# A four-block vision kernel on one core: normalisations of three chunks merged, another order in the third pass, and three products by high and low parts

## What is computed

```python
xn = layernorm(x, ln1_w, ln1_b)
xs = jnp.roll(xn, shift=(-SHIFT, -SHIFT), axis=(1, 2))      # SHIFT = 3
xw = xs.reshape(B, H // WS, WS, W // WS, WS, C)             # windows of WS x WS = 7 x 7 = 49 tokens
xw = xw.transpose(0, 1, 3, 2, 4, 5).reshape(-1, N, C)
qkv = xw @ qkv_w + qkv_b
qkv = qkv.reshape(-1, N, 3, NH, hd).transpose(2, 0, 3, 1, 4)   # 6 heads of 16
q, k, v = (qkv[0], qkv[1], qkv[2])
attn = jax.nn.softmax(jnp.einsum('bhqd,bhkd->bhqk', q, k) * scale, axis=-1)
o = jnp.einsum('bhqk,bhkd->bhqd', attn, v)
o = o.transpose(0, 2, 1, 3).reshape(-1, N, C)
o = o @ proj_w + proj_b
...
x = shortcut + o
h = layernorm(x, ln2_w, ln2_b)
h = jax.nn.gelu(h @ mlp_w1 + mlp_b1, approximate=False)     # 96 -> 384 -> 96
x = x + (h @ mlp_w2 + mlp_b2)
```

## Time and profile before

| | us |
|---|---|
| median of 3 runs | 12922.99 |
| lowest, highest | 12919.95, 12924.1 |
| the profiled execution: its own time | 12924.79 |
| the profiled execution: span of the trace | 12922.7 |
| its mean granted PE clock | 0.985 of full |

### The profile page before, as it was taken

One profiled execution on the slowest core, in us unless ns is written; L12 is line 12 of the kernel. 1 busy time (PEld: TensorE's weight loads), 2 busy tenths in 40 slices (PEclk: granted clock), 3 DMA queues, 4 the chain that ended last, 5 costly groups with the idle time before them and its releaser, 6 DMA issues. The chain is left out here.

```text
span 12922.7 us, 343424 instructions
## 1 busy us (share of the span) xinstructions
PE 11843.0 (92%) x135956; PEld 7144.1 (55%) x135956; DVE 7256.5 (56%) x12102; ACT 8898.6 (69%) x15550; POOL 308.8 (2%) x772
## 2 busy tenths in 40 slices
PE   6999998999999999999888888888899999999999
PEld 3444443555555555556755555555566666666665
DVE  4444444666666666663455555655555555555555
ACT  4555554888888888884355555555677777777777
POOL 0000000000000000000000000000000000000000
PEclk9999998999999999999999999999899999999999
DMA  1111111222222222225522222222000000000000
...
DMA packets 1103863, 593.29 MB, mean 46 GB/s; under 512 B 864651, under 2 KB 1076566, under 8 KB 1099704
## 3 DMA queue, kind: packets, MB, share of 16 engines
...
...
## 5 line engine op out<-in xcount | busy, mean ns | idle before, releaser
L964 PE MATMUL banks<-L_VB,L_PT 113*49 113x34 f32 x36864 | 1086.4, 214 | 294.5 <-ACT L_PT L1117 294.5
L964 PEld LDWEIGHTS banks<-L_VB,L_PT 113*49 113x49 f32 x36864 | 1007.1, 126 | 618.1 <-issue 618.1
L913 PEld LDWEIGHTS banks<-L_ident,L_PR 113*113 113x113 f32 x9216 | 1116.8, 179 | 340.9 <-issue 246.9
L913 PE MATMUL banks<-L_ident,L_PR 113*113 113x113 f32 x9216 | 1280.0, 270 | 3.2 <-ACT L_PR L1133 2.6
L985 PE MATMUL banks<-L_XN,L_W 97*128 97x392 f32 x3072 | 1243.5, 514 | 3.2 <-ACT L_Y L1164 1.5
L908 PE MATMUL banks<-L_SQ,L_J 96*96 96x392 f32 x2560 | 1095.6, 509 | 142.6 <-ACT L_SQ L1106 142.6
L1117 ACT COPY L_PT<-banks 113x452 f32<-113x452 f32 x1792 | 947.2, 529 | 375.4 <-PE banks L913 369.0
L378 PE MATMUL banks<-scan_XS,scan_W1T 97*96 (+1 forms) x2688 | 1112.4, 552 | 0.0
L1133 ACT ACTIVATE L_PR<-L_SX 113x588 f32<-113x588 f32 x1536 | 1088.6, 709 | 16.4 <-DVE L_SX L1260 10.7
L1057 PE MATMUL banks<-L_Hd,L_W 128*97 128x392 f32 x3072 | 1099.1, 493 | 0.0
L1111 ACT ACTIVATE L_LV<-banks,L_eps 96x392 f32<-96x392 f32 x1280 | 747.1, 584 | 430.5 <-PE banks L908 430.5
...
## 6 DMA issues: line engine op xcount, KB each, us to landing
...
after_L<-L_X SPq DMA_DIRECT2D x512, 147.0 KB
...
L_norm_by_phase<-L_XP SPq DMA_DIRECT2D x512, 84.0 KB, 2.2
...
L_norm<-L_XA SPq DMA_DIRECT2D x256, 147.0 KB, 2.0
...
L_XR<-L_norm SPq DMA_DIRECT2D x256, 147.0 KB, 2.2
```

What stands on the lines that cost most here:

```text
L913: mm = pe.transpose(bank(TURN[a])[0:SPAN, (k % 4) * SPAN:(k % 4 + 1) * SPAN], PR[:, st.v if lag else st.u, 2 * k:2 * k + 2, :].rearrange(" ...
L964: mm = pe.matmul(bank(HEADS_BANK)[p0:p0 + TOK, col:col + VW], PT[:, st.v, q // 2 * G + g, p0:p0 + TOK], VB[:, st.v, q, g, :], start=True, ...
```

## The change

1. The normalisations of a step are merged. `variances` multiplies the squares of chunk t+1 (X), t-2 (X1) and, in L1, t-3 (X2) by a 96 x 32 `J`, in pieces of 98 columns, and leaves each mean on 32 rows of its own of one bank; ACT takes one Ln and one Exp of all of them (`rstd`); `spread` multiplies each group of 32 rows by `PICK` (one row of ones) and puts it on 96 rows of three banks; DVE multiplies from there (`normalised`). XN is thus made one step ahead.
2. The squares go from ACT to POOL (`square_rows`, and SQ2 and SQ3 in `step`), and so does XA. POOL runs now in L3 too.
3. Keys, queries and the first MLP layer are computed by parts: x and the weights are each split into a high part, rounded to the format float32r, and the rest; three float32r matmuls (high x high, high x low, low x high) add up in the bank. The weights are split once (`split_weights`), the activations by POOL: a cast and a subtraction each for XN and XN2. The convolution pass had such matmuls already.
4. The order of the steps of L1 and L3 is another one: heads come ahead of the hidden blocks, keys and queries at the step's start, values behind `spread`.
5. In L2 DVE adds both halves of the bias first, and the second subtraction comes behind the sums; on PE the second and third `turn` stand together ahead of the values, the turned heads no longer wait for the queries' copy and come ahead of the convolution's product, and the scores wait for `biased1` in place of `centred1`; ACT copies both PT groups ahead of the values.

```diff
+def split_weights(nc, name, parts):
+            @block.vector
+            def _(dve):
+                for whole, high, low in parts:
+                    dve.tensor_copy(high.bitcast(F32R), whole).then_inc(rounded, 1)
+                dve.wait_ge(rounded, len(parts))
+                for whole, high, low in parts:
+                    dve.tensor_tensor(low.bitcast(F32R), whole, high, ALU.subtract)
...
-                def variance(sq, k, ready):
-                    pe.matmul(bank(k)[0:C, 0:CH], J[:], sq, start=True, stop=True).then_inc(s[ready], 1)
+                def norms(st):
+                    nx = st.ahead()
+                    return ([(0, SQ[:, nx.u])] if nx.f else []) + ([(1, SQ2[:, st.u])] if st.m else []) + ([(2, SQ3[:, st.v])] if st.n and kind == "L1" else [])
+                def variances(st):
+                    if st.ahead().f:
+                        st.ahead().wait("sq", 0)
+                    if st.m:
+                        st.wait("sq2", 2)
+                    if st.n and kind == "L1":
+                        st.wait("sq3", 3)
+                    if st.k:
+                        st.wait("centred1", 1)
+                    for k in range(PAIRS):
+                        cols = slice(2 * TOK * k, 2 * TOK * (k + 1))
+                        for g, sq in norms(st):
+                            mm = pe.matmul(bank(VAR_BANK)[NORM_ROWS * g:NORM_ROWS * (g + 1), cols], J[:], sq[:, cols], start=True, stop=True)
+                    mm.then_inc(s["variances"], 1)
+                def spread(st):
+                    st.wait("rstd", -1)
+                    for k in range(PAIRS):
+                        cols = slice(2 * TOK * k, 2 * TOK * (k + 1))
+                        for g, _ in norms(st):
+                            rows = slice(NORM_ROWS * g, NORM_ROWS * (g + 1))
+                            mm = pe.matmul(bank(NORM_BANK[g])[0:C, cols], PICK[rows], RS[rows, st.u, cols], start=True, stop=True)
+                    mm.then_inc(s["spread"], 1)
...
+                def by_parts(out, wh, wl, xh, xl):
+                    for n, (wt, xt) in enumerate(((wh, xh), (wh, xl), (wl, xh))):
+                        mm = pe.matmul(out, wt.bitcast(F32R), xt.bitcast(F32R), start=(n == 0), stop=(n == 2))
+                    return mm
...
+                    out = bank(K_BANK)[0:C, 0:CH]
                     if mlp:
-                        st.wait("centred1", 1)
-                    pe.matmul(bank(K_BANK)[0:C, 0:CH], Wk[0:C + 1, :], XN[:, st.u], start=True, stop=True).then_inc(s["k"], 1)
...
                 def hidden(st, j):
-                    pe.matmul(bank((7, 6, 7)[j])[:, 0:CH], W1[0:C + 1, j * 128:(j + 1) * 128], XN2[:, st.u],
-                              start=True, stop=True).then_inc(s[f"fc1_{j}"], 1)
+                    cols = slice(j * 128, (j + 1) * 128)
+                    by_parts(bank((7, 6, 7)[j])[:, 0:CH], W1H[0:C + 1, cols], W1L[0:C + 1, cols], XN2H[:, st.u], XN2L[:, st.u]).then_inc(s[f"fc1_{j}"], 1)
...
+                        st.wait("xn_parts", 0)
+                        keys(st)
+                    if st.k:
+                        st.wait("probs0", 1)
+                        turn(st, 0)
+                    if st.f:
+                        if st.n:
+                            st.wait("x2", 3)
+                        queries(st)
+                    if normed:
+                        variances(st)
...
+                        turn(st, 2)
+                    if normed:
+                        spread(st)
...
+                        st.wait("xn2_parts", 2)
...
+                def rstd(st):
+                    present = [g for g, there in enumerate((st.ahead().f, st.m, st.n and kind == "L1")) if there]
+                    whole = present == list(range(len(present)))
+                    parts = [slice(0, NORM_ROWS * len(present))] if whole else [slice(NORM_ROWS * g, NORM_ROWS * (g + 1)) for g in present]
+                    st.wait("variances", -1)
+                    for rows in parts:
+                        ins = act.activation(LV[rows, st.u], bank(VAR_BANK)[rows, 0:CH], ACT.Ln, bias=eps[rows, 0:1])
+                    ins.then_inc(s["lv"], 1)
+                    st.wait("lv", -1)
+                    for rows in parts:
+                        ins = act.activation(RS[rows, st.u], LV[rows, st.u], ACT.Exp, scale=-0.5)
+                    ins.then_inc(s["rstd"], 1)
...
+                def normalised(st):
+                    nx = st.ahead()
+                    st.wait("spread", -1)
+                    if st.m:
+                        dve.tensor_tensor(XN2[0:C, st.u], X1[0:C, st.u], bank(NORM_BANK[1])[0:C, 0:CH], ALU.mult).then_inc(s["xn2"], 1)
+                    if nx.f:
+                        nx.wait_turn(loaded[nx.of4(0)], 0, N_LOADS, 4)
+                        dve.tensor_tensor(seen(XN[0:C, nx.u]), win(X[0:C, nx.of4(0)]), win(bank(NORM_BANK[0])[0:C, 0:CH]), ALU.mult).then_inc(s["xn"], 1)
+                    if st.n and kind == "L1":
+                        st.wait("xa", 5)
+                        dve.tensor_tensor(XH[:, st.v], X2[0:C, st.v], bank(NORM_BANK[2])[0:C, 0:CH], ALU.mult).then_inc(s["xh"], 1)
...
                 def mlp_step(st):
+                    normed = st.t < last_norm if st.static else True
+                    if st.f:
+                        keys(st)
                     if st.k:
                         pt_copy(st, 0)
                     if st.f:
-                        st.wait("rstd", 0)
-                        dve.tensor_tensor(seen(XN[0:C, st.u]), win(X[0:C, st.of4(0)]), win(RS[:, st.u]), ALU.mult).then_inc(s["xn"], 1)
-                    if st.m:
-                        st.wait("rstd2", 2)
...
                         values_odd(st)
+                    if normed:
+                        normalised(st)
...
                 def attention_step(st):
                     if st.f:
+                        bias(st, 0)
+                        bias(st, 1)
                         centre(st, 0)
-                        centre(st, 1)
+                        row_maximum(st, 1)
                     if st.k:
                         over_sums(st)
+                    if st.f:
+                        subtract(st, 1)
                     if st.k:
                         residual(st)
...
+                    def square_rows(st, lag):
+                        c = st.t - lag
+                        pool.wait_ge(loaded[st.of4(lag)], (c // 4 + 1) * (16 * N_LOADS))
+                        held(st, "variances", lag + 2)
+                        u = st.v if lag % 2 else st.u
+                        pool.tensor_tensor(SQ[:, u], X[0:C, st.of4(lag)], X[0:C, st.of4(lag)], ALU.mult).then_inc(s["sq"], 1)
+                    def split_rows(st):
+                        held(st, "xn", 0)
+                        pool.tensor_copy(XNH[:, st.u].bitcast(F32R), XN[:, st.u]).then_inc(s["xn_high"], 1)
+                        held(st, "xn_high", 0)
+                        pool.tensor_tensor(XNL[:, st.u].bitcast(F32R), XN[:, st.u], XNH[:, st.u], ALU.subtract).then_inc(s["xn_parts"], 1)
                     def step(st):
-                        if st.n:
-                            st.wait("xa", 3)
+                        if st.n and kind == "L1":
+                            st.wait("variances", 1)
+                            held(st, "x2", 3)
+                            pool.tensor_tensor(SQ3[:, st.v], X2[0:C, st.v], X2[0:C, st.v], ALU.mult).then_inc(s["sq3"], 1)
+                        if not st.static or st.t + 2 < NCH:
+                            square_rows(st, -2)
+                        if st.m:
+                            held(st, "xn2", 2)
+                            pool.tensor_copy(XN2H[:, st.u].bitcast(F32R), XN2[:, st.u]).then_inc(s["xn2_high"], 1)
+                            held(st, "xn2_high", 2)
+                            pool.tensor_tensor(XN2L[:, st.u].bitcast(F32R), XN2[:, st.u], XN2H[:, st.u], ALU.subtract).then_inc(s["xn2_parts"], 1)
+                        if st.ahead().f:
+                            split_rows(st.ahead())
+                        if st.n and kind == "L1":
...
+                        if st.k:
+                            st.wait("variances", 0)
+                            held(st, "x1", 1)
+                            pool.tensor_tensor(SQ2[:, st.v], X1[0:C, st.v], X1[0:C, st.v], ALU.mult).then_inc(s["sq2"], 1)
```

251 lines of the change are left out of this document (129 added, 122 removed).

## The result

The changed kernel takes **14201.09 us** (median of three, 14194.45 to 14205.2) against 12922.99: a ratio of 1.0989, 95% interval 1.0964 to 1.1014. It is slower by 1278 us; 12750 was forecast, and the range ended at 13110.

A forecast was written before the change was run, and what follows sets the result against it. PE's own order was taken to bound L1 and L3, while in L2 PE waits for others. L2 -450, L1 +270 and L3 0 sum to -180, perhaps 5 added for the prologue: 12750 us, range 12540 to 13110.

The forecast's parts named there:

- The new chains of L1: L1: two dependency chains through POOL's split of XN2 set a step of 15.4 us, losing 270 us.
- chain A: L1, X2's end to next X2's end through the load of X (5.5 us), POOL's square and split: 15.2 us.
- Chain B: L1, X2's end to next X2's end through POOL's SQ3, `variances`, `spread`, normalisation and split: 15.15 us.
- L3: 0 (-60 to +130 us): L3: the step stays at 14.8 us, so no gain or loss, within -60 to +130 us.
- L2: 8.2 forecast: L2: the new order removes the heads' wait for the PT copy; step 9.95 to 8.2 us, gaining 450 us.
- DVE's regrouping: L2: biases added first and second subtraction moved shorten DVE's chain to the heads; step 8.6 us if it gives nothing.
- Rival 4: L2: another wait replaces the PT copy's, so the step is 9.2 us and the whole 13000; 11%.
- POOL's prices: POOL in L1 and L3: 1.0 us for a two-input operation with semaphore, 0.55 for the cast.
- Rivals 1 and 3: POOL's two-input operations: 1, slower than taken, gain gone from 1.23 us (25%); 3, a copy's 0.54, whole 12480 (13%).
- Rival 2: L1 and L3: the narrow matmuls of `variances` and `spread` do not overlap, +870 us, whole 13600; 6%.
- The parts: PE in L1 and L3: a product by parts costs 0.6 us for 0.75; five gain 0.75 us a step.
- its own list of what to look for in the trace: Signs expected after: L2 near 8.2, L1 near 15.4 with PE idle 1.5 to 2 us ahead of the first hidden block.

The follow-up runs named there:

- e6: The changed kernel with the store of X2 a step later and, on DVE, the normalisation ahead of the odd values' copy: 12389.17 us.
- e1: The changed kernel with three needless float32 matmuls more in each step of L1, ahead of the first hidden block: 13192.63 us.
- e2: The changed kernel with SP's store of X2 in L1 issued one step later, so the load of X no longer stands behind it: 13574.03 us.
- e4: The changed kernel with L3's `variances` and `spread` as one matmul of 392 columns per group in place of four of 98: 13775.67 us.
- e3: The changed kernel with L1's first MLP layer in float32 on whole XN2, without POOL's split of XN2 there: 12353.42 us.

## Why the prediction was wrong

**The step that failed** is the end of "The new chains of L1": PE "stands still some 1.8 us ahead of the first hidden block", and then a step of 15.4 made of durations of the earlier trace rows. I had PE's idle time as a consequence and priced it as time alone; that the durations behind it are only good at the clock they were read at was never asked. In the step shown above PE runs at 1.2 GHz from 3025.95 to 3036.09, 10.14 us; e6, with the same code on PE, has 5.70 from the same matmul to the same matmul at 2.4 GHz (3008.86 to 3014.56). Over the 700 us of L1 the stretch takes 8.5 to 10.2 us, 9.7 in the mean, so the clock costs 4.0 a step: 19.98 - 4.0 = 16.0. The stretch lies in both chains, so all of it counts. L1 was forecast at +270 and is +1444 by its mean step; the clock's part is about 1020.

**A term that was too small** is the load in chain A, 5.5 us. In the step above X2 ends at 3016.78 (3016.15 + 0.63), SP issues the load at 3020.73 and POOL begins the square at 3023.41: 6.6, and 6.2 to 6.8 in the other steps. That makes A 16.0 or so, and is most of what is left between 15.4 and 16.0, some 155 us. e1, with A uncut and a clock of 0.98, agrees: most of its steps in L1 take 15.8 to 17.1. Chain B was right: 15.15 forecast, 15.1 to 15.4 in the steps of e2 that kept their clock. The wait ahead of the hidden block was 2.3 to 3.1 for 1.8; e2 shows that one of 1.9 would have lost the clock as well in most steps.

**The second step** is "L3: 0 (-60 to +130 us)". Its row was right: undisturbed steps take 14.6 (e4), 14.8 forecast, with 0.76 of waiting for the split where 0.15 was allowed. What I had nothing for is that 24 records in a step (that many fewer, and it is gone) make the loop's body one that is loaded in every turn, with PE waiting for it and losing its clock behind the second stall: +361.

Point by point:
- L2: 8.2 forecast, 8.02 measured; -450 forecast, -494 by step, -508 alone on the chip. It is just under the least that I had allowed, 8.05: DVE's regrouping gave all that I had hoped for. The 508 hold also what the clock cost in 11 of 239 steps before, which the one step that I read did not have. Rival 4 fell.
- POOL's prices: 1.0 for a two-input operation with its semaphore, 0.55 for the cast; 0.84 for the square, 1.01 for the subtraction, 0.51 for the cast. Rivals 1 and 3 fell.
- `variances` and `spread`: 0.95 each; 0.88 and 0.93. Rival 2 fell.
- The parts: 0.6 for a product by parts; three matmuls are 0.175 apart, but the first of a product takes 0.26 to 0.48, so that a pair of hidden blocks is 1.26 where I had 1.2, and keys to the turn 0.83. The gain of 0.75 from five products was 0.47 in L3, and in L1 nothing that the step can use.
- Chains A and B: forecast at 15.2 and 15.15, they are 16.0 and 15.3 at 2.4 GHz. Either alone is long enough to leave PE waiting for 1.9 us or more, so both have to be cut (e6), or the split that they share (e3).
- The sum: from -180 to +1278 are 1458. The clock in L1 makes 1020 of it, the loading in L3 361, the load of X 155, and L2 gave 58 more than forecast: 1478.

None of the rivals was the clock, although the prediction wrote down the cause, idle time in every step, and its own list of what to look for in the trace named it. The trace of before had a sign of it too: the steps of L2 in which a wait of 1.15 us halved the clock.
